# Relative-position attention and a gated low-rank layer on one core: where the products of values and probabilities stand among the query groups

## The reference

```python
qk = jnp.einsum('bhld,bhrd->bhlr', q, k) / np.sqrt(HEAD_DIM)
qk = qk + jnp.einsum('bhld,lrd->bhlr', q, rel)      # rel = rel_emb[r - l + 511]
att = jax.nn.softmax(qk, axis=-1)
out = jnp.einsum('bhlr,bhrd->bhld', att, v)         # 16 heads of 16
...
x = x + layernorm(attention(layernorm(x)))
x = x + layernorm(ffn(layernorm(x)))                # base + shared + top 2 of 6 routed rank-16 parts
```

## Time and profile before

| | |
|---|---|
| median of 3 runs | 6519.43 us (6518.75 to 6520.47) |
| the profiled execution | 6501.09 us, of which the span from the first to the last instruction is 6499.3 us |
| mean granted TensorE clock | 0.990 |
| TensorE matmul, weight load | 6203.9 us (95%), 5783.0 us (89%) |
| VectorE, ScalarE, GpSimd | 77%, 48%, 56% |

### The profile page before, as it was taken

How to read it: one execution, slowest core, us unless ns; L and a number is a source line. 1 busy time by engine, 2 the same in 40 slices (tenths; PEclk the granted TensorE clock), 3 DMA queues, 4 the chain that set the end, 5 groups by cost and what they waited for, 6 DMA issues and landing times.

```text
span 6499.3 us, 408509 instructions
## 1 busy us (share of the span) xinstructions
PE 6203.9 (95%) x178176; PEld 5783.0 (89%) x178176; DVE 5036.1 (77%) x10289; ACT 3134.0 (48%) x5145; POOL 3640.9 (56%) x4707
## 2 busy tenths in 40 slices
PE   5999999999999999999999999999999999999997
PEld 4999899999999999999999999899999999998997
DVE  3777777777787777777777777777777777777776
ACT  2444444444444444444444444444444444444444
POOL 5555555555565555555555555555555555555555
PEclk8999999999999999999999999999999999999998
DMA  3111121111212112121111211112111121211210
GB/s 86 37 44 50 37 58 37 51 45 35 58 36 59 35 35 61 35 60 33 42 56 35 60 36 48 45 39 58 35 52 43 35 58 38 59 35 33 62 35 27
DMA packets 570089, 296.73 MB, mean 46 GB/s; under 512 B 384176, under 2 KB 534688, under 8 KB 568624
## 3 DMA queue, kind: packets, MB, share of 16 engines
q1 hardware_dynamic: 568624, 272.86, 15.2%
HBM read 184.46 MB, written 88.60 MB: 42 GB/s over the span
## 4 chain that ended last, share of the span: by engine, by line
PE 75%; DVE 15%; issue 6%; DVEq 3%; POOLq 1%; POOL 0%; SPq 0%; ACT 0%; DMA 0%
PE sc L665 19%; PE sc L681 13%; PE sc L660 11%; PE pw L691 11%; DVE r L960 6%; PE pm L672 6%; PE pm L712 4%; PE pw L698 4%; PE pw L712 4%; DVE nm L969 3%; DVE ceq L1008 2%; DVEq L971 2%; DVE y2n L926 1%; DVE dm L983 1%; PE pm L703 1%
## 5 line engine op out<-in xcount | busy, mean ns | idle before, releaser
L960 DVE TRANSPOSE_TENSOR_REDUCE r<-sc 128x32 f32<-128x1024 f32 x2048 | 2547.5, 1244 | 49.2 <-PE sc L665 48.3
L665 PE MATMUL sc<-rm,tw 96*128 96x32 f16 x65536 | 2288.9, 176 | 58.1 <-issue 58.1
L845 ACT ACTIVATE prob<-sc 128x1024 f32<-128x1024 f32 x2048 | 2095.7, 1023 | 237.9 <-PE sc L681 173.7
L665 PEld LDWEIGHTS sc<-rm,tw 96*128 96x128 f16 x65536 | 1976.9, 97 | 64.7 <-issue 64.3
L660 PE MATMUL sc<-qm,ks 96*128 96x64 f16 x32768 | 1635.2, 193 | 29.9 <-DMA ks<-qk_s 15.1
L969 DVE TENSOR_REDUCE nm<-pm 16x32 f16<-16x256 f32 x2048 | 840.5, 410 | 932.2 <-PE pm L672 931.4
L660 PEld LDWEIGHTS sc<-qm,ks 96*128 96x128 f16 x32768 | 1380.8, 98 | 105.7 <-issue 35.2
L681 PE MATMUL sc<-nmm,pick 128*128 128x64 f16 x32768 | 1305.7, 194 | 1.4 <-DVE nmm L972 1.4
L681 PEld LDWEIGHTS sc<-nmm,pick 128*128 128x128 f16 x32768 | 1150.9, 98 | 126.9 <-issue 103.2
L691 PE MATMUL pw<-prob,vs 128*32 128x128 f32 x32768 | 1110.2, 276 | 100.2 <-DVE nm L969 89.9
L691 PEld LDWEIGHTS pw<-prob,vs 128*32 128x32 f32 x32768 | 835.2, 110 | 158.5 <-DVE nm L969 119.8
(11 more groups left out here) (129 smaller groups left out, 5753.9 us busy)
## 6 DMA issues: line engine op xcount, KB each, us to landing
raw<-qk_s SPq DMA_DIRECT2D x774, 64.0 KB, 2.5
tw<-tw_s SPq DMA_DIRECT2D x512, 72.0 KB, 2.0
v_s<-vpad SPq DMA_DIRECT2D x136, 256.0 KB, 3.4
vs<-v_s SPq DMA_DIRECT2D x64, 512.0 KB, 3.7
ks<-qk_s SPq DMA_DIRECT2D x384, 64.0 KB, 2.4
xin<-x SPq DMA_DIRECT2D x138, 128.0 KB, 2.1
qk_s<-qkh SPq DMA_DIRECT2D x272, 64.0 KB, 1.7
qk_s<-qkl SPq DMA_DIRECT2D x272, 64.0 KB, 1.6
```

Source lines behind the costliest of these rows:

```text
L665: last = mm(out3[:, :, 2 * k:2 * k + 2], tw[:, jp, u:u + P], rm[:, i, k, :, :], start=False, stop=False, skip_group_check=True)
L845: A(prob[:, jp % 2, :, :, i * IW:(i + 1) * IW], sc[:, 2 * buf:2 * buf + 2, :].rearrange("p c (h i) -> p c h i", i=IW), ACT.Exp).then_inc(s ...
L960: v.tensor_reduce(r1[:, :], sc[:, 2 * buf:2 * buf + 2, :].rearrange("p c (h i) -> p (c h) i", i=IW), axis=AX.X, op=ALU.max, apply_transpos ...
```

## The change

`pv` loses its argument `half` and makes all four columns in one call. The call of step k = 1 now makes all 32 products and increments `s_pv`; the call in step k = 2 is gone. Nothing else changes, and no wait is moved apart from that of `s_pv`, which is satisfied a step earlier.

```diff
-            def pv(jp, half):
+            def pv(jp):
 
-                for col in (2 * half, 2 * half + 1):
+                for col in range(4):
                     for c in range(2):
                         for q in range(4):
...
-                        pv(pj, 0)
-                    elif k == 2:
-                        pv(pj, 1).then_inc(s_pv, 1)
-                    else:
+                        pv(pj).then_inc(s_pv, 1)
+                    elif k == 3:
                         transpose_parts(t * NJP + jp - 1)
```

## The result

The changed kernel takes 6598.91 us in the median of 4 runs (6598.12 to 6612.24), the kernel before 6519.56 us: a ratio of 1.0126, 95% interval 1.0109 to 1.0144 (the two medians alone give 1.0122). It is 79 us slower. The profiled execution has a span of 6596.8 us, 97.5 us above that of the first profile of before. Part of that difference is chance: a second profile of the kernel before, taken later, has a span of 6513.7 us.

What follows compares the result with a forecast made beforehand. TensorE, busy 95% of the span, was taken as the bound, so only its idle time could change. Per tile −0.30 − 0.01 + 0.06 + 0.80 = +0.55 us, 69 us over 126 tiles: 6519.4 to 6588 us, range 6500 to 6635.

Steps and rivals of the forecast that it cites:

- The sum of the pairs: Net change of the four merged step pairs: +0.55 us a tile, 69 us over 126 tiles.
- Pair 2: Steps 9 to 11: 0.88 us added, 0.89 given back, so −0.01 us a tile.
- the rival for a faster kernel: The array alone decides: 0.13 us saved a pair, 66 us faster, 6454 us; chance 0.04.
- Pair 0: Steps 1 to 3: nmm of step 2 ends just after GpSimd's subtraction; 0.09 us lost, +0.06 on average.
- The part on the first tile of a pass: Steps 1 to 3: GpSimd stands elsewhere in a loop pass's first tile, so the loss there is nothing.
- Pair 3: Steps 13 to 15: step 14's nmm, held under GpSimd's qm, is no longer covered by products; +0.80 us a tile.
- the rival without a hold: Step 14's nmm not held under qm: step 15's mark 0.19 us late, tile 0.24; 6510 us; chance 0.13.
- Pair 1: Steps 5 to 7: longer step 5 hides step 6's 0.81 us wait for nm, gate delay swallowed; −0.30 us a tile.
- the second rival: The rival without a hold: 6510 us, some 9 us less with Pair 1's full 0.37 us gain; chance 0.13.
- the rival of the late gate: Step 6: ceq starts too late, nm up to 0.5 us late; 63 us more, 6651 us; chance 0.07.
- The rival of a falling clock: Step 14's wait lowers the granted clock, at most 176 us over all tiles, 6764 us; chance 0.03.
- what was costed at nothing: ScalarE's moved copy of products, later nm copy and gate exponential, and the transfers of values: no time added.

Runs made afterwards that it cites:

- The split of pair 3: Changed kernel with products merged in pairs 0, 1 and 2 and left in two halves in pair 3: 6502.76 us, ratio 0.9976 to the kernel before.
- the gated kernel: Kernel before with GpSimd's first masking put ahead and its maskings of groups 1 and 2 waiting for nmm: 6512.41 us, ratio 1.0002.

## Why the prediction was right, point by point

The forecast was 6588 us, the time 6598.9; +1.1% against +1.2% by the medians. The sum of the pairs was forecast at +0.55 us a tile and is +0.64.

Step k = 1 grows by 8 rounds of 110 ns: right, 4.05 to 4.06 us in steps 5, 9 and 13 in the mean, against 4.06 said. Step 1 is 4.05 to 4.06 us too, but 4.54 in the first tile of a pass.

Step 10 at 2.37 us, the length of the chain: right to 0.01 us. Pair 2 came out at −0.04 instead of −0.01. The array's own gain, the rival for a faster kernel, is there in the loads (0.14 us of idle time in step 10), but VectorE's chain takes it: the run with pairs 0 to 2 merged is not measurably faster than that with pair 1 alone.

Pair 0: +0.07 measured, +0.06 said. In the tile of the trace nmm of step 2 ends at 3140.07, 0.04 us after GpSimd's subtraction, and the step is 2.44 us, where 2.45 were forecast. The part on the first tile of a pass was wrong, and it is luck that it hardly matters: put at nothing, steps 1 and 2 lose 0.10 us there, and 0.07 in the other tiles, where 0.09 was said.

Pair 3, the nmm held under qm: right in mechanism and size, +0.79 against +0.80. The hold was to cost 0.58 us of it (0.77 less the 0.19 of the rival without a hold), and with the masking moved ahead step 14 is 0.59 us shorter. The split of pair 3 shows that the whole loss sits there. The rival that nmm would not be held is refuted by its 0.76 us. Of y2n I had said that it would be 0.32 us shorter once it was off the mask: it was 0.31 (0.69 to 0.38).

Pair 1: the mechanism, the wait of the products for nm hidden behind a longer step 5, was right, and its size was off: −0.18 us a tile and not −0.30. The step that failed is the one in brackets, "I take that the delay is swallowed there". ceq did become shorter (0.20 us for 1.00), but the exponential came so late that `gate`, the operation ahead of it, met the subtraction and ended with it, and ceq, cgt and nm came behind that. nm was 0.17 us later than said. Putting the exponential first brings step 6 to the forecast's 2.37 us, and pair 1 then gains 0.36 us a tile; the 0.37 us that the second rival calls the full gain has no working in the prediction, but is near this. So the rival of the late gate held in part: 0.12 us × 126 = 15 us. Pair 2, 0.03 us a tile better than said, takes 4 of them back, and what is left is the 11 us that the forecast lacks.

The rival of a falling clock is refuted: step 14's loads wait 0.90 us, and the mean granted clock is that of the kernel before, 0.988. Of what was costed at nothing, ScalarE's order is what mattered, by the gate's exponential; the copy of the products cost nothing that shows (steps 3 and 11 are within 0.02 us of before).

The sum was made against an execution 18 us shorter than the median. That did no harm, since only differences of steps went into it, but the span of that profile alone would have made the change look like 97 us.

## What to carry to other kernels

Work that stands in a wait is not idle filler: before moving it, ask of the step it leaves how long its dependency chain is without cover, and whether it had a wait of its own that a longer step ahead of it hides. Here only one pair in four had one, and merging there alone, with the one ScalarE operation that the merged block delayed taken out of its way, gave 0.6%, while merging everywhere cost 1.2%. Read such a chain together with the operations that GpSimd runs beside it, and check a reordering on GpSimd at the next place where the two meet, and not only at the one it is meant for.

## What the runs showed of the hardware that I had not expected

How much hangs on who comes first between VectorE and GpSimd. A VectorE operation of 0.18 us took 1.07 us because a masking operation had started 0.12 us ahead of it, and such meetings in two steps of a tile cost 164 us over the kernel; a wait of GpSimd for nmm brought the time back, with xn still held. In the changed kernel with the masking ahead, GpSimd's addition of x1 ended 0.02 us before nmm began (3148.36 and 3148.38), and nmm was not held. Not only operations with two tensor inputs are held: `gate`, a multiplication of 6 numbers a partition by a scalar, took 0.57 us for 0.23, and xn, of 256 numbers, 1.37 us for 0.37. What decides where two masking operations follow each other is not shown: in the kernel before xn starts 0.14 us ahead of the end of the first (3131.55, 3131.69) and is let in between them, and the second takes 1.28 us for 1.15; in the gated kernel it starts 0.11 us ahead of the end of the first and is held through the second.

The idle 0.20 us behind the four-strip products is the same behind 32 and behind 64 records. By the rule of the Trainium skill's "TensorEngine Tiling (Array Packing)", section "Key Properties", changing the tiling mode drains the array. The traces agree that 0.20 us are paid once for each such burst; that they are this drain no run here shows. Saving one of two was worth nothing that the runs can tell, since the step that saves it is then as long as VectorE's chain.
